# Moving the flag load, the first exponential's table and the fourth head copies in a two-block perceiver kernel

## The reference

```
x = x + L0_xattn(ln(x), ctx)   # ternary weights, int8 activations, two short attentions
x = x + L0_attn(ln(x))         # rope, 16 query heads on 4 key heads, causal, within 32 tokens
x = x + L0_ffn(ln(x))          # gate mixes 8 experts into W1 and W2; gelu
x = x + L1_xattn(ln(x), ctx)   # "long attention": 16 heads of 8, 512 keys for every sample
x = x + L1_attn(ln(x))         # 16 heads, causal, within 32 tokens
x = x + L1_ffn(ln(x))          # one linear map in the frequency domain
```

## Time and profile before

| | |
|---|---|
| median of 3 runs | 361.68 us (361.33 to 361.83) |
| profiled execution | 361.33 us |
| its span | 359.5 us |
| PE busy | 282.0 us, 78% |
| DVE busy | 239.4 us, 67% |
| ACT busy | 174.9 us, 49% |
| POOL busy | 58.9 us, 16% |
| TensorE clock granted, mean | 0.906 of full speed |

### The profile page before, as it was taken

The page is one execution under the profiler, slowest core; times in us unless marked ns, Lnnn a source line. Parts: engine busy times, 40 slices in busy tenths (PEclk is TensorE's granted clock), DMA queues, the critical chain, the costliest instruction groups (busy, mean ns, idle before and its releaser), DMA issues.

```text
span 359.5 us, 7808 instructions
## 1 busy us (share of the span) xinstructions
PE 282.0 (78%) x3060; PEld 170.6 (47%) x3061; DVE 239.4 (67%) x570; ACT 174.9 (49%) x316; POOL 58.9 (16%) x182
## 2 busy tenths in 40 slices
PE   0029494879998899599999996757999999867954
PEld 0013431434463578464445553245566666643842
DVE  4699898975879968449733445585476777436744
ACT  3769695974446664440100000435587787721440
POOL 3033050800000021020002001222222222202102
PEclk9999678898999999989999999667699999995995
DMA  6990000000002999591000000000000000000000
GB/s 166 253 366 4 1 0 2 1 2 1 2 4 41 209 222 232 158 391 31 1 0 0 0 2 0 0 1 0 5 4 5 4 5 5 6 2 1 4 2 29
DMA packets 6320, 19.41 MB, mean 54 GB/s; under 512 B 1156, under 2 KB 2692, under 8 KB 5252
## 3 DMA queue, kind: packets, MB, share of 16 engines
q1 hardware_dynamic: 6277, 18.82, 19.2%
HBM read 12.07 MB, written 0.26 MB: 34 GB/s over the span
## 4 chain that ended last, share of the span: by engine, by line
PE 55%; DVE 29%; ACT 5%; DMA 4%; issue 3%; SPq 2%; POOL 0%; DVEq 0%; ACTq 0%
PE PS L1095 51%; DVE sm L734 5%; DMA cx<-ctx_in 4%; DVE yq L741 3%; DVE big L794 3%; PE PS L1284 2%; DVE w L897 2%; DVE sm L896 1%; DVE yq L985 1%; DVE yq L803 1%; ACT sa L422 1%; SPq L269 1%; DVE tern L982 1%; ACT xT L531 1%; ACT xT L422 1%
## 5 line engine op out<-in xcount | busy, mean ns | idle before, releaser
L1049 DVE TENSOR_REDUCE sm<-PS 128x1 f32<-128x512 f32 x64 | 42.9, 689 | 25.8 <-PE PS L1095 23.2
L587 ACT ACTIVATE yq<-PS,sm 128x512 f32<-128x512 f32 x44 | 29.8, 687 | 10.0 <-PE PS L1095 9.2
L322 POOL TENSOR_TENSOR rstd<-veps,mhalf 128x1 f32<-128x1 f32 x24 | 12.6, 549 | 134.5 <-DVE veps L622 134.5
L422 ACT ACTIVATE big<-PS,cols,sm 128x512 f32<-128x512 f32 (+1 forms) x40 | 32.3, 872 | 1.3 <-PE PS L1095 1.2
L1095 PE MATMUL PS<-sa,w 128*32 128x36 f32 (+1 forms) x320 | 30.8, 280 | 2.4 <-ACT w L554 2.4
L1095 PE MATMUL PS<-yq 128*128 128x384 f32 x96 | 31.1, 486 | 0.0
L1095 PE MATMUL PS<-diag,ones 128*128 128x128 f32 x14 | 4.6, 424 | 33.6 <-DVE diag L667 24.6
L1095 PE MATMUL PS<-big,yq 96*128 96x512 f16 x64 | 26.3, 417 | 5.2 <-DVE sm L1049 2.5
L1095 PE MATMUL PS<-yq,big 99*128 99x128 f16 x256 | 26.1, 226 | 5.5 <-issue 2.3
L531 ACT COPY xT<-PS 128x512 f32<-128x512 f32 x5 | 2.9, 588 | 51.1 <-PE PS L1284 51.1
L1095 PEld LDWEIGHTS PS<-yq,big 99*128 99x128 f16 x256 | 17.5, 101 | 18.1 <-issue 15.5
(11 more groups left out here) (246 smaller groups left out, 577.6 us busy)
## 6 DMA issues: line engine op xcount, KB each, us to landing
big<-yq SPq DMA_DIRECT2D x24, 256.0 KB, 5.4
cx<-ctx_in SPq DMA_DIRECT2D x8, 384.0 KB, 11.2
w<-w_in SPq DMA_DIRECT2D x9, 256.0 KB, 4.7
yq<-w_in SPq DMA_DIRECT2D x1, 2304.0 KB, 10.8
wa<-wa_in SPq DMA_DIRECT2D x1, 1156.0 KB, 18.6
sa<-wx_in SPq DMA_DIRECT2D x1, 768.0 KB, 14.6
rows<-rows_in SPq DMA_DIRECT2D x1, 580.0 KB, 16.2
tern<-rows_in SPq DMA_DIRECT2D x1, 512.0 KB, 8.7
```

The lines of the kernel that those rows point to most:

```text
L322: pool.tensor_tensor(rstd[:, t:t + 1], veps[:, t:t + 1], mhalf[:, t:t + 1], ALU.pow)\
L422: return nc.scalar.activation(o, i, func, bias=bias, scale=scale, **kw)
L587: nc.scalar.activation(pt(i), PS[:, ST_BANK[i % 2], :], ACT.Exp, scale=s1(M_ES))\
L1049: V.tensor_reduce(s1(M_MX + i % 8), PS[:, S_BANK[i % 3], :], AX, ALU.max, negate=True)\
```

## The change

The change makes four edits.

- DVE's clear of `diag`, its wait for the flag and its load move from behind the head copies of the queries to ahead of them, behind `add_bias`. PE's wait and load move from behind the query products to ahead of the transposes of layer norm 3.
- After the last Gelu ACT takes the exponential of one column of zeros into an unused column of `sm` (column 19).
- The head copies of queries by POOL go. ACT makes the copies of heads 2 and 3, and its evacuations and copies are put in a new order: evacuation 0 and 1, copies 0, evacuation 2, copies 1, evacuation 3, copies 2, copies 3. PE waits for two ACT copies per group and no longer for POOL.
- In both self attentions POOL's copy of the keys goes, and DVE makes the copies of heads 0, 1 and 3.

```
# POOL
-            def last_keys_head(k):
-                pool.wait_ge(s["k_plain"], k + 1)
-                pool.tensor_scalar(kexp[:, 3, :], mix[:, :], hm[:, 3:4], 1.0, ALU.mult, ALU.mult).then_inc(s["k_evp"], 1)
...
-            last_keys_head(0)
...
-            for r in range(R):
-                pool.wait_ge(s["lq_low"], r + 1)
-                pool.tensor_scalar(head_queries(r, 3), split_queries(r), hm[0:96, 3:4], 1.0, ALU.mult, ALU.mult)\
-                    .then_inc(s["lq_e3"], 1)
...
-            last_keys_head(1)
# ACT
+            nc.scalar.activation(s1(M_EXP0), s1(M_Z4), ACT.Exp)
             rows_to_features(3)
-            for r in range(R):
+
+            def long_queries(r):
                 act.wait_ge(s["lq_ps"], r + 1)
                 affine(kexp[:, r, :], PS[:, r, :], scale=s1(M_BE), bias=s1(M_BQS + r)).then_inc(s["lq_ev"], 1)
-            for r in range(R):
+
+            def last_heads(r):
                 act.wait_ge(s["lq_low"], r + 1)
-                affine(head_queries(r, 2), split_queries(r), scale=hm[0:96, 2:3]).then_inc(s["lq_e2"], 1)
+                for h in (2, 3):
+                    affine(head_queries(r, h), split_queries(r), scale=hm[0:96, h:h + 1]).then_inc(s["lq_e2"], 1)
+
+            long_queries(0)
+            long_queries(1)
+            last_heads(0)
+            long_queries(2)
+            last_heads(1)
+            long_queries(3)
+            last_heads(2)
+            last_heads(3)
# DVE
-                for h in (0, 1):
+                for h in (0, 1, 3):
                     V.tensor_scalar(kexp[:, h, :], mix[:, :], hm[:, h:h + 1], None, ALU.mult).then_inc(s["k_evd"], 1)
...
             add_bias(R_BO)
+            link(V.memset(diag[:, 64:128], 0.0))
+            dve.wait_ge(s["flag_ok"], 1)
+            in_bounds = dve.value_load(flags[0:1, 0:1], min_val=0, max_val=1)
             for r in range(R):
...
-            link(V.memset(diag[:, 64:128], 0.0))
-            dve.wait_ge(s["flag_ok"], 1)
-            in_bounds = dve.value_load(flags[0:1, 0:1], min_val=0, max_val=1)
# PE
-                pe.wait_ge(s["k_evd"], 2 * k + 2)
+                pe.wait_ge(s["k_evd"], 3 * k + 3)
                 pe.wait_ge(s["k_eva"], k + 1)
-                pe.wait_ge(s["k_evp"], k + 1)
...
+            pe.wait_ge(s["flag_ok"], 1)
+            in_bounds = pe.value_load(flags[0:1, 0:1], min_val=0, max_val=1)
             rows_to_features(3, xn)
...
-            pe.wait_ge(s["flag_ok"], 1)
-            in_bounds = pe.value_load(flags[0:1, 0:1], min_val=0, max_val=1)
...
-                    pe.wait_ge(s["lq_e2"], r + 1)
-                    pe.wait_ge(s["lq_e3"], r + 1)
+                    pe.wait_ge(s["lq_e2"], 2 * r + 2)
```

More of the change, by code:

```diff
@@ L149, in perceiver @@
         rm = cst[:, C_RM:C_RM + 4]
+        M_EXP0 = 19
         M_V, M_G, M_SI, M_INV = 0, 20, 30, 40
@@ L231, in perceiver @@
                  "kv_off_ps", "kv_mm", "kv_ev", "sc_ps", "sc_max", "sc_exp", "sc_tp", "sc_tev", "sc_teva", "pv_ps", "pv_read",
-                 "f1_in", "f1_tp", "f1_qT", "f1_ps", "f1_ev", "f2_qd", "f2_qa", "f2_ps", "x_up", "x_tile", "x_done", "k_plain", "k_evp",
+                 "f1_in", "f1_tp", "f1_qT", "f1_ps", "f1_ev", "f2_qd", "f2_qa", "f2_ps", "x_up", "x_tile", "x_done", "k_plain",
                  "xt_ps", "xt_ev", "xrep_ok", "qk_ps", "q_ev", "k_evd", "k_eva", "v_ps", "v_ev", "vones", "sa_ps", "sa_sub", "sa_exp",
@@ L236, in perceiver @@
                  "kp_ps", "kp_h", "kp_l", "vp_ps", "bound_in", "bound_ps", "scales_ok", "root_in", "root",
-                 "lq_ps", "lq_ev", "lq_low", "lq_e", "lq_e2", "lq_e3", "key_ones", "ls_ps", "ls_max", "ls_parts", "ls_rows_ps", "ls_rows", "lt_raw", "lt_clipped",
+                 "lq_ps", "lq_ev", "lq_low", "lq_e", "lq_e2", "key_ones", "ls_ps", "ls_max", "ls_parts", "ls_rows_ps", "ls_rows", "lt_raw", "lt_clipped",
                  "lt_ps", "lt_exp", "lo_ps", "lo_cp", "lo_tp", "lo_norm", "lo_ev", "v_ones",
```

## The result

The changed kernel takes 357.18 us in the median of 4 runs (355.8 to 357.93); the kernel before, on the same chip, 361.73 (361.33 to 361.83). The ratio is 0.9872, with a 95% interval from 0.9835 to 0.9908: 4.5 us faster, where 2.8 were forecast, and inside the range. The profiled execution after is the longest of its four (357.93 us, span 356.1), the one of before the shortest of its own, so the two traces differ by only 3.4 us; what follows accounts for those 3.4.

The account below looks back on a forecast made before the run. The prediction took a chain of waits to bound the kernel, chiefly at the start of the long attention's score loop. Gains of 2.3 + 0.4 + 0.1 = 2.8 us took 361.33 to 358.5 us, range 355.8 to 360.3.

Parts of the forecast that it names:

- Flag: Start of the long attention's score loop: DVE's clear and load move to idle time, taking 1.64 us off the path.
- Head copies: Queries of the long attention: without POOL beside it a DVE pair takes 0.61 us instead of 1.06.
- POOL as the cause: Query head copies: POOL slows DVE's copies; the rival that it doesn't gave 359.2 to 360.3 us, chance 0.13.
- The term of 2.3 us: Start of the long attention: flag and query copies together bring `scores(3)` 2.0 to 2.8 us earlier, taken as 2.3.
- First exponential: Long attention: with the table load moved behind the last Gelu, it starts when its scores are ready, 0.4 us earlier.
- The rival of a pause behind the load: At the first exponential: the table switch holds up more than its row shows, 1.4 us more gain, 357.1; chance 0.01.
- Key copies: Self attentions: three unhindered DVE copies end under PE's mask products; 0.1 us gained in the first, 0 in the second.
- The rival that the clock comes up earlier: PE's run behind `scores(3)`: full clock by 240.35, gain 4.7 us in place of 2.3, 356.1 in all; chance 0.24.
- signs of being wrong: ACT's last copy after 239; products behind `scores(3)` in another clock, up to 2.4 us either way; DVE pairs at 1.06.
- The give-back: PE's thin stretch, 250 to 254 us: longer low clock eats the gain; no change, chance 0.06, or slower, 0.04.
- the sum: Whole kernel: 2.3 for flag and query copies, 0.4 for the exponential, 0.1 for the keys, 2.8 us in all.

Follow-up runs that it names:

- the spare POOL copies: All four edits, with POOL again copying the queries four times into memory nobody reads, against the kernel before: 357.5 us, ratio 0.9948.
- the spare products at the start: All four edits plus PE products nobody reads, before layer norm 3's transposes and before scores 0 to 2, against the kernel before: 353.17 us, ratio 0.9825.
- the spare products at the end: All four edits plus PE products nobody reads, only behind the long attention up to around layer norm 4, against the kernel before: 352.38 us, ratio 0.984.
- Head 3 on DVE: All four edits, but DVE copies head 3 of the queries and ACT only head 2, against the kernel before: 354.27 us, ratio 0.9866.
- the trace of both: All four edits, DVE copying head 3 of the queries, and unread PE products from layer norm 3 to scores 2, against the kernel before: 354.55 us, ratio 0.9888.
- the first group: Four kernels with one edit each against the kernel before, on one chip; the kernel before has a median of 360.51 us there.

## Why the prediction held, and where its size was off

**Flag.** Right. 1.64 us were to leave the path; alone it gave 1.79 at `scores(3)`, and the issue gap is gone. Neither load appears on the chain at its new place.

**Head copies.** Right, with POOL as the cause, which the spare POOL copies show. The pairs take 0.61 us, ACT's order ends at 237.90 (forecast 238.10), `scores(2)` goes at 236.74 (236.8), the first maximum stands at 237.11 (237.25 to 237.3), and `scores(3)` at 238.41 (238.1 to 238.9). The term of 2.3 us measured 2.85 behind the copy of `xT`.

**First exponential.** Right: 0.4 forecast, 0.45 in the trace of that edit alone and 5.22 - 4.81 = 0.41 in the whole. The rival of a pause behind the load falls with it.

**Key copies.** 0.1 to 0.15 forecast, 0.17 in the trace, nothing in the time. The prediction's reading of the 1.42 us, the longest key copy of before, was incomplete: that copy ends at 137.53, and POOL's head copy at 136.75, but POOL goes on with two clears until 137.25. In the second self attention, with no clears behind POOL's copy, it takes 0.92. So the clears seem to hold DVE up as well, which no run tests.

**The clock, the mis-sized term.** The forecast left PE's 6.74 us behind `scores(3)` as they were. From `scores(3)` to the copy of `cx` they went from 6.77 to 4.81 us. The rival that the clock comes up earlier, at a chance of 0.24, is what happened at this place: it gave 4.7 us at that point, and 4.81 came, though its parts came out otherwise: it had `scores(3)` at 238.9 and 4.1 us behind it, where 238.41 and 4.81 were measured. It had the clock up by 240.35; the low stretch ends between 240.4 and 241. The measured median lies in the range given to this rival (355.5 to 357.5) and not in that of the forecast (357.7 to 359.2), and PE's products in another clock behind `scores(3)` stood among the prediction's own signs of being wrong. In the traces with the flag or the queries alone this interval takes 5.96 and 5.98 us, so each edit shortens the low stretch in part: it lasts 10.2 us with neither (three traces), 6.8 with one of them (two), 3.4 with both (three). That the clock is the reason, the spare products at the start show: with no low clock there, the interval takes 4.0 us.

**The give-back.** The prediction had a rival for it, but in the wrong place. It looked at the thin stretch of 250 to 254, whose low clock lasts as long as before (6.5 us). Instead 2.13 us went back in the second self attention, 80 us on, in code that the change hardly touches. That the first 1.12 of them are the clock, the spare products at the end show; for the other 1.01 it is likely and not shown. So what came is not the 2.8 us of the sum: in the traces it is 5.2 us by the first exponential, less what went back later. Neither the 2.0 us that the clock gave behind `scores(3)` nor the 2.1 lost in the second self attention were in the sum, and that they nearly cancel, so that the time came within 1.3 us of the forecast, is luck.

**Left open.** Why the clock falls where it does in one execution and not in another: in the trace with POOL beside, no row between 231 and 309 us shows it low, in the same program stage where the changed kernel has two low stretches. Head 3 on DVE and the spare products at the start, each good alone, are together no better, and the clock accounts for part of that: the trace with head 3 on DVE already has full clock from 229.3 to 314.7 us, so the spare products have no low stretch left to remove there, and the trace of both is low again from 247.6 to 251.0 and from 309.1 to 312.5. Its first exponential is 0.7 us earlier than with head 3 on DVE alone, its `xT` copy for layer norm 4 1.8 us later. Why the clock falls there is open; and whether the kernel before would have gained as much from spare products in the right place, which wasn't tried.

## What to carry to other kernels

Look at the head of a loop for register loads and table loads that stand between the last producer and the first consumer; moved to a place where the engine idles anyway they cost nothing. What that gains is how long the consumer waited for the load and nothing else: all 1.64 us of the flag's load and clear here, but 0.4 to 0.5 of the 1.28 of the table load, since the scores weren't ready earlier. Where GpSimd copies beside VectorE out of SBUF, read VectorE's least and most duration of one instruction form: a factor of two between them is time that comes back when GpSimd's copy goes elsewhere, and it counts where VectorE is on the path (1.51 us at the queries, nothing to be measured at the keys). A gap of PE costs a second time where the clock falls behind it, so work out a removed gap at both clocks, look for stages behind it that may fall in turn, and try spare products in the gaps that are left, ahead of the waits and never behind them.

## What the runs showed of the hardware beyond this

One kernel's executions on one chip, the kernel before in the first group, run from 355.47 to 362.21 us (30 runs), a spread larger than the change; their mean granted clock goes from 0.905 to 0.929. The Trainium skill ("TensorE: Matmul & The Clock Gate", Part 1: The HAM clock gate) calls the number of slow products at the start of a kernel variable from run to run. Two traces of the changed kernel show that of a later stretch: at layer norm 3 (223.3 to 226.3 us) the clock is 1.00 in the first and 0.50 in the second, while their other low stretches agree. And the same head copy takes VectorE 0.35 us and ScalarE 0.72 (0.61 and 1.32 for a pair).
